# A chunked RWKV-7 block: the pair matrices from 64-column matmuls, and new written orders for the engines

## The reference

```python
xn = _layernorm(x)
s = attn(xn)                      # RWKV-7 time mixing
g = _silu(ffn(xn))                # ffn: down(silu(gate(xn)) * up(xn)), 256 -> 768 -> 256, int weights / 127
return x + s * g
```

```python
sa = einsum('bhij,bhj->bhi', S, at)
S = S * dt[:, :, None, :] + sa[..., None] * bt[:, :, None, :] + vt[..., None] * kt[:, :, None, :]
y = einsum('bhij,bhj->bhi', S, rt)
```

## Time and profile before

| | |
|---|---|
| median of 3 runs | 1602.91 us (1601.87 to 1603.78) |
| the profiled execution's own time | 1603.78 us |
| its span, first to last instruction | 1602.3 us |
| TensorE busy | 1493.2 us (93%) |
| VectorE busy | 1261.4 us (79%) |
| ScalarE busy | 1073.9 us (67%) |
| GpSimd busy | 335.8 us (21%) |
| mean granted TensorE clock | 0.982 |

### The profile page before, as it was taken

One profiled execution on the slowest core, in us unless ns is written; L12 is line 12 of the kernel. 1 busy time (PEld: TensorE's weight loads), 2 busy tenths in 40 slices (PEclk: granted clock), 3 DMA queues, 4 the chain that ended last, 5 costly groups with the idle time before them and its releaser, 6 DMA issues.

```text
span 1602.3 us, 56437 instructions
## 1 busy us (share of the span) xinstructions
PE 1493.2 (93%) x24384; PEld 1028.5 (64%) x24384; DVE 1261.4 (79%) x2661; ACT 1073.9 (67%) x1889; POOL 335.8 (21%) x362
## 2 busy tenths in 40 slices
PE   3579999999999999899999989999999999999977
PEld 1256767576676767667676666757666675766755
DVE  2788888888888888788887878888888888878623
ACT  3658587585858758576775858768585876858412
POOL 3020301313040131302213030131304013130101
PEclk9799999999999999999999999999999999999979
DMA  4011120301112030110302112030111203011110
GB/s 149 14 21 21 35 47 17 62 19 40 28 35 47 17 62 19 33 34 24 58 16 46 35 21 47 17 62 19 40 36 32 42 17 62 20 40 28 34 34 28
DMA packets 251462, 58.37 MB, mean 36 GB/s; under 512 B 223696, under 2 KB 250704, under 8 KB 251088
## 3 DMA queue, kind: packets, MB, share of 16 engines
q1 hardware_dynamic: 241936, 41.95, 13.8%
q10 hardware_dynamic: 9280, 12.81, 2.2%
HBM read 36.38 MB, written 18.35 MB: 34 GB/s over the span
## 4 chain that ended last, share of the span: by engine, by line
PE 85%; DVE 6%; issue 2%; DMA 2%; ACT 2%; POOL 1%; SPq 1%; ACTq 0%; DVEq 0%; POOLq 0%
PE bank L536 21%; PE chunk L380 15%; PE bank L546 10%; PE bank L511 4%; PE bank L666 3%; PE chunk L644 3%; PE chunk L616 3%; PE chunk L591 3%; PE chunk L600 3%; PE bank L479 2%; PE bank L519 2%; PE bank L485 2%; DMA smalls<-in_x 2%; PE chunk L630 2%; PE bank L380 2%
## 5 line engine op out<-in xcount | busy, mean ns | idle before, releaser
L1327 POOL TENSOR_TENSOR SF<-ST,CT 128x256 f32<-128x256 f32 x128 | 84.1, 657 | 678.3 <-DVE ST L1213 678.3
L536 PE MATMUL bank<-xT,wg 128*128 128x256 f32 x768 | 202.8, 396 | 13.4 <-DVE VU L983 13.4
L536 PE MATMUL bank<-xT,wu 128*128 128x256 f32 x768 | 201.7, 395 | 4.6 <-DVE hT L1173 4.6
L546 PE MATMUL bank<-wd,hT 128*128 128x256 f32 x768 | 177.2, 384 | 0.9 <-DVE hT L1173 0.9
L536 PEld LDWEIGHTS bank<-xT,wg 128*128 128x128 f32 x768 | 139.2, 191 | 58.7 <-DVE VU L983 24.0
L546 PEld LDWEIGHTS bank<-wd,hT 128*128 128x128 f32 x768 | 144.5, 192 | 27.7 <-issue 7.4
L536 PEld LDWEIGHTS bank<-xT,wu 128*128 128x128 f32 x768 | 139.2, 191 | 34.1 <-issue 7.9
L380 PE MATMUL chunk<-KS,W 128*128 128x512 f32 x320 | 151.1, 603 | 2.3 <-ACT gT L721 2.3
L863 ACT ACTIVATE sg<-bank 128x512 f32<-128x512 f32 x96 | 57.2, 595 | 137.3 <-PE bank L536 125.6
L889 ACT ACTIVATE Y<-chunk 32x256 f32<-32x256 f32 x256 | 96.0, 375 | 50.1 <-PE chunk L600 47.3
L380 PE MATMUL chunk<-big,W 128*112 128x512 f32 (+1 forms) x256 | 121.9, 600 | 2.9 <-POOL big L1286 2.6
(11 more groups left out here) (157 smaller groups left out, 3230.1 us busy)
## 6 DMA issues: line engine op xcount, KB each, us to landing
smalls<-in_x SPq DMA_DIRECT2D x32, 256.0 KB, 3.0
Y<-in_x SPq DMA_DIRECT2D x32, 256.0 KB, 3.0
out<-fsil ACTq DMA_DIRECT2D x32, 256.0 KB, 2.2
scrA<-AM SPq DMA_DIRECT2D x64, 64.0 KB, 1.9
hat<-scrB SPq DMA_DIRECT2D x32, 128.0 KB, 3.1
hat<-scrF SPq DMA_DIRECT2D x32, 128.0 KB, 3.3
KE<-scrA SPq DMA_DIRECT2D x64, 32.0 KB, 2.1
scrT<-KE SPq DMA_DIRECT2D x16, 128.0 KB, 1.7
```

Of the source, the lines that this page charges most:

```text
L536: q = pe.matmul(o[:, TT_ * n2:TT_ * n2 + TT_], w[:, h, 128 * (n + n2):128 * (n + n2) + 128], x_now[:, h], start=(h == 0), stop=(h == NH - 1))
L546: q = pe.matmul(o[:, 256 * m:256 * m + 256], hT[:, n, 128 * m:128 * m + 128], wd[:, n, :], start=(n == 0), stop=(n == NF - 1))
L1327: pool.tensor_tensor(SF[:, :, :, :], ST[:, :, :, :], fade[:, c].unsqueeze(3).to_broadcast([128, B, NH, N]), ALU.mult).then_inc(*faded.up)
```

## The change

In `pairs` the loop over the kind x goes, and one matmul takes the 64 columns of block j (both kinds of keys) as weights, so its output covers 64 partitions of the batch's half. The columns of K past 8j + 8 of each kind, which hold what earlier blocks or quarters left there, are multiplied too, and the mask leaves these places out as it did before. All three orders of PE, ACT and DVE are new, of POOL the string ORDER is new and the other two are as before; each string has the same number of each letter.

```diff
-ORDER = {"pe": ("NNNFNKOOFNNOKVONNNNKVKRRBKBNNRNNNBBNBBVBNNBVBBNBBEBNBBVBBNBBVBXBBNNBXBBNBBXBXBBNBBNBXBBXNBBLBXBBNXBB"
-                "LXXXXLL"),
-         "act": ("NFKFFFFFOFNNKVKOVKKKBERBKKXRRXDBXBNNVBVBBVVBNBBXBBBVXBBBVNBXBBXBBLBXLBLBBXNBBLXX"),
-         "dve": ("ONBOOBBBBBOBBDBBBBDBBDDBNBBOKKXFEDKDDDKNEEXKEEXBBXXNXBXXBXXXBXXXBEEXXBXXXXBNLBXBLXXBXBXXNXXXXXXBXBXB"
-                "LLXBBXLLLLLLLL"),
-         "pool": ("DBBBBBLBLBBBLLLLLLLL")}
+ORDER = {"pe": ("NNNFNKOOFNNORVNNNNKKOVKRBNKBNRNNVBBNBBNBNBNBBVNNBBEBVBBNBBVBNBBNBBXBXBBNXBBNBNBBXBBXBXBBNBBLBNBBXXBB"
+            "LXXXXLL"),
+         "act": ("NFKFFFFFRFVNKKNVOKKKBEBOKRKRDXXBXBVNBVNBBVVNBBBXBVVBBXBBBBNBBXXBLBBXLXBXBBNBBLXX"),
+         "dve": ("ONBOOBBBBBDBBBBBBBNBBDBBDDOOKKDXEFKKNDEDEXDKEEBXBXXXNBXBXXXBEXXBEXXBXNXBLXBXXXBXXBLXBXNXXXBXXXBXLXLBX"
+             "XXBBXXLLLLLLLL"),
+         "pool": ("DBBBBBBLBBLBLLLLLLLL")}
...
-LAST = {"pe": ("NNNNNONONNNOONNNBBNNNBBNBBBBBNBBBBBBNBBBBNBBBBBBNNBBBBBNBBBBNBBBBBBNBBNNNN"),
+LAST = {"pe": ("NOOONONNNNNNNNNBBNNNBBBBBNBBBBBNBBBBBNBBBBBNBBBNBBNBBBBBNBBBBBNBBBNBBNNNNN"),
...
-        "dve": ("BONOOBBBBBBBBBBBBBBBBONONBBBBBBBBNBBBNBBBBBNB"),
+        "dve": ("BOOOBBBBBBBBBBBBBBBBONONNBBBBBBBBBBBNBBBBBNBN"),
...
@@ -505,11 +505,9 @@
                     for n in range(QC // 2):
                         for j in range(NJ):
                             for b in range(B):
-                                for x in range(2):
-                                    p0, keys = 64 * b + L * x, BL * j + BL
-                                    oc = o[p0:p0 + keys, 128 * n:128 * n + 128].rearrange("p (x e) -> p x e", e=L)
-                                    q = pe.matmul(oc[:, :, BL * j:BL * j + BL], K[:, 2 * n + b, 64 * j + L * x:64 * j + L * x + keys],
-                                                  Q[:, 2 * n + b, j, :, :, :].rearrange("p a b e -> p (a b) e"), start=True, stop=True)
+                                oc = o[64 * b:64 * b + 64, 128 * n:128 * n + 128].rearrange("p (x e) -> p x e", e=L)
+                                q = pe.matmul(oc[:, :, BL * j:BL * j + BL], K[:, 2 * n + b, 64 * j:64 * j + 64],
+                                              Q[:, 2 * n + b, j, :, :, :].rearrange("p a b e -> p (a b) e"), start=True, stop=True)
                         if n == 1:
                             yield f"half{qt}"
                     q.then_inc(*ring.fill((t, "A", qt)))
```

More of the change, by code:

```diff
@@ L51 @@
 CTOT = _at
-ORDER = {"pe": ("NNNFNKOOFNNOKVONNNNKVKRRBKBNNRNNNBBNBBVBNNBVBBNBBEBNBBVBBNBBVBXBBNNBXBBNBBXBXBBNBBNBXBBXNBBLBXBBNXBB"
-                "LXXXXLL"),
-         "act": ("NFKFFFFFOFNNKVKOVKKKBERBKKXRRXDBXBNNVBVBBVVBNBBXBBBVXBBBVNBXBBXBBLBXLBLBBXNBBLXX"),
-         "dve": ("ONBOOBBBBBOBBDBBBBDBBDDBNBBOKKXFEDKDDDKNEEXKEEXBBXXNXBXXBXXXBXXXBEEXXBXXXXBNLBXBLXXBXBXXNXXXXXXBXBXB"
-                "LLXBBXLLLLLLLL"),
-         "pool": ("DBBBBBLBLBBBLLLLLLLL")}
-FIRST = {"pe": ("NNFKFVKKVNKNNRNNNRVKNNNNVNNNNVVREXNNXXXLXXNNXXNNXNLNNXXXLNLNN"),
-         "act": ("FKFFNFFFNKFNKNVVKKEKRVVVNKXDKRXVRXVXLVNXNLXLXXXXLNX"),
-         "dve": ("DNDDDDKKEDNDFDNKKNEENXXLKXEXXEXXEXXXXXXELXXXXXXXXXXXXXXXXNXXLLXXXXXLLLLLLLL"),
+ORDER = {"pe": ("NNNFNKOOFNNORVNNNNKKOVKRBNKBNRNNVBBNBBNBNBNBBVNNBBEBVBBNBBVBNBBNBBXBXBBNXBBNBNBBXBBXBXBBNBBLBNBBXXBB"
+            "LXXXXLL"),
+         "act": ("NFKFFFFFRFVNKKNVOKKKBEBOKRKRDXXBXBVNBVNBBVVNBBBXBVVBBXBBBBNBBXXBLBBLXLBXBBNBBLXX"),
+         "dve": ("ONBOOBBBBBDBBBBBBBNBBDBBDDOOKKDXEFKKNDEDEXDKEEBXBXXXNBXBXXXBEXXBEXXBXNBXLBXXXBXXBLXBXNXXXBXXXBXLXLBX"
+             "XXBBXXLLLLLLLL"),
+         "pool": ("DBBBBBBLBBLBLLLLLLLL")}
+FIRST = {"pe": ("NFKFKKNNNNNVNNKVRKRVNRVVNNNNNNNNNNNNNNNNNVEXXXNXXXLXXXXXLXLLN"),
+         "act": ("NNKFFFNFNNFFKFKVKKKEVKKRRXXDRVVVVVVXXXNNXNLXXLLXXLX"),
+         "dve": ("DNDDDNFKKEDNKKDXEXDDENKEXXXLEXXXXXXLXXXEXEXXXXXXXXNXXXXXXXXXXXLLXXLLLLLLLNL"),
          "pool": ("DLLLLLLLLLL")}
-LAST = {"pe": ("NNNNNONONNNOONNNBBNNNBBNBBBBBNBBBBBBNBBBBNBBBBBBNNBBBBBNBBBBNBBBBBBNBBNNNN"),
-         "act": ("NNNBBOBBBBOBBNBBBBBBBBNBNBBBBBBBBBNBN"),
-         "dve": ("BONOOBBBBBBBBBBBBBBBBONONBBBBBBBBNBBBNBBBBBNB"),
-         "pool": ("BBBBBBBBB")}
+LAST = {"pe": ("NOOONONNNNNNNNNBBNNNBBBBBNBBBBBNBBBBBNBBBBBNBBBNBBNBBBBBNBBBBBNBBBNBBNNNNN"),
+        "act": ("NONNOBBNBBBBBBBBNBBBBBBBBBNBBBBBBBBNN"),
+        "dve": ("BOOOBBBBBBBBBBBBBBBBONONNBBBBBBBBBBBNBBBBBNBN"),
+        "pool": ("BBBBBBBBB")}
 NB = 4
```

## The result

The changed kernel takes 1608.76 us (median of 10 runs, 1604.13 to 1614.75), the kernel before 1599.9 us beside it (10 runs, 1595.47 to 1605.19). The ratio is 1.0053, 95% interval 1.0037 to 1.0069: slower by 0.5%, some 8.5 us. The direction was forecast, but 45 us of it were expected, and 1608.76 lies outside the range of 1632 to 1662.

The account below looks back on a forecast made before the run. TensorE (PE), busy 1493.2 of 1602.3 us, was taken as the bound. 1603.8 + 44.9 (pair matmuls) + 1.5 (tile 0) - 1.5 (orders) = 1648.7 us, against the median 1648 us; range 1632 to 1662 us.

Parts of the forecast that it names:

- the round: Pair matmuls: records running side by side, four per 33 ns before, forecast two per 58 ns with 64 weight columns.
- The twin at line 573: Corner product with 32 records, two strips and 64 weight columns; its 1.11 us was taken as the new half's length.
- the half: Pair matmuls of half a quarter, 8 per tile: alone 0.74 us before, 1.11 us forecast.
- Rival B: Pair matmuls: the round stays at 33 ns, so no change, 1603 us; 3 in 100.
- time added to or taken from a PE stage in the steady sections passes to the end nearly one for one: Steady sections: 2.99 us more matmul time in each of 15 sections was to give +44.9 us.
- rival A: Pair matmuls: a price for each record makes the half 0.27 us, total 1571 or 1591 us; 7 in 100.
- 30.7 us of idle time: PE's free time in 1200 us of steady sections, about 2.4 us a section, taken to bound the new orders' gain.
- rival D: Group norm on VectorE meets GpSimd's mixes in five sections more, some 4 us each: 1668 us; 7 in 100.
- I take -1.5 us over all: Written orders of all four engines: the longer last row of two covers 0.77 us of each of two group-norm waits.
- nothing within 3 us: Last section, which has no pairs: its new order was taken as worth nothing, within 3 us.
- 65 changes of shape: PE's steady order: 65 changes of matmul shape before and afterwards, each costing a like drain, so no effect.
- C: Steady sections: the new orders close all PE idle time and hide the longer halves, 1612 us; 3 in 100.

Follow-up runs that it names:

- experiment 1: The changed kernel's 64-column matmuls with all written orders of the kernel before: 1624.37 us, ratio 1.0134 to the kernel before.
- experiment 5: Changed kernel with one old string each: ORDER 1614.17 us, FIRST 1612.61, LAST 1619.18; kernel before with new ORDER alone: 1646.99 us.

## Why the prediction was wrong

**Right.** PE bounds the kernel. 64 weight columns set the round at 58 ns for two records. The twin at line 573 gave the half to 0.01 us (1.11 forecast, 1.12 measured), and two experiments moved the round with the columns (29 ns at up to 32, 48 ns in the mean of 40 to 64). LDWEIGHTS lasts 138 ns where 133 was forecast. Rival B, a round that stays at 33 ns, is out. The direction, slower, was right.

**The step that failed: "time added to or taken from a PE stage in the steady sections passes to the end nearly one for one".** It was shown wrong by experiment 1: +44 us of stage time gave +21. The largest part of what is missing that the traces can assign is what the removed records had cost elsewhere: the narrow halves used up PE's fetched instructions. Of the 20 stalls, 3 stood inside the pairs and their transposes and 17 in the recurrence stages behind them. The sum had put this at nothing. I had priced the instruction count only inside the half, in rival A, where it costs nothing. The trace before held the signs, in the same view as the earlier trace rows, of which I had used only the waits for VectorE:

```profile
PE chunk L630 <- issue: 3.5, 7, 0.9
...
PE chunk L600 <- issue: 1.4, 3, 0.8
PE bank L511 <- issue: 0.7, 1, 0.7
```

None of these stages begins with such a wait for data; it stands in their middle. A gap shorter than the 0.2 us that a matmul's record lasts is hidden as busy time, so that 30.7 us of idle time was no bound on what PE could win back. Of the 26.1 us that experiment 1 wins back in 14 sections of the traces (42.1 less 16.0), stalls of over 0.18 us are 10.6 and the group norm's waits 5.8. Behind one of these waits, of 2.7 us, the clock before fell to half its level:

```profile
671.00:679.00 8.00, 8.00 (x31) 4.71 (x30) 5.30 (x18) 5.25 (x7) 0.00 (x0) 0.57 0.21 66
```

The stages from line 420 to the next of line 666 took 7.3 us there, and the same stages 4.1 us in the trace of experiment 1. Another 3.0 us lie ahead of line 644, which in the trace before waits for VectorE's VU for 2.4 us in five places. The last 3.5 us are not assigned.

**The group norm's wait** in the steady sections was part of the profiled execution before and of none of the twelve others, with old or new orders (rival D's mechanism, in the other direction). One trace can't tell whether every execution of the kernel before has it. My forecast started from a median of 1602.9 us for three runs, where ten gave 1599.9: 3 us of the 39 us error.

**"I take -1.5 us over all" for the orders.** They are worth 1.0134 - 1.0053, 13 us, and by the times the largest part lies in FIRST and LAST, which I had put at nothing within 3 us. That is the second failed term. Some 6 of the 13 us, by the estimate of experiment 5, are a higher clock outside the steady sections, which the prediction did not price at all. ORDER, which I had called neutral by its 65 changes of shape, is neutral within the intervals when the matmuls are wide. I also miscounted it: the new string has two rows of two halves in a section, since half2 and matrix2 are adjacent too, which saves one switch, 0.2 us. The prediction's last paragraph would have put an error with halves as forecast on the orders, to be seen in PE's waits for other engines. The larger part was in the matmuls after all, and its sign was the waits that went.

**The sum as it was:** 1600 + 44 (halves) - 23 (stalls, waits, clock and gaps that went) - 13 (orders) = 1608 us, against 1608.76 measured. The 23 is the 44 less experiment 1's 21, so that the sum must come out; measured by themselves in the traces are 10.6 us of stalls, 5.8 of waits and 3.2 of clock.

**The rivals.** A was wrong as put: the half did not get shorter with its record count. But a price for records was there, outside the half: 10.6 us of stalls. C named the place where a part of the time went (PE's idle time) and held it to be 36 us; 1612 us was its figure, nearer than the forecast. That was luck: it needed every wait of the earlier trace rows gone, and the 10.7 us for the mixes are all still there, with 17.3 of the 30.7 free us.

## What to carry to other kernels

When PE is busy for 97% of a stretch, look for waits marked "issue" in the middle of its stages before pricing a change in the number of matmuls: the instructions have to be fetched, and a dense burst of small matmuls is paid for where the block ends, in the burst or in the stage behind it. Counting PE's records modulo 256 finds the place. Busy time made of overlapping records hides every gap shorter than one record; sum the times from start to start instead. A written order belongs to the matmuls it was made with: the same strings were worth -13 us with one form of the matmuls and +32 us with the other, so test them as a pair.

## What the runs showed of the hardware beyond this

PE resumed 1.2 to 1.6 us after the landing of a 16 KB block of instructions in 19 of 20 gaps of the kernel before, and 1.61 us after it in the twentieth. The blocks themselves took 0.9 to 1.9 us, mostly about 1, and in the thirteen traces none started sooner than 3.2 us after the last. By the count of records, PE had at most some 300 records in hand when the fetch of a block began (212 in the median before), so the fetch was about one block ahead of it. A round of two records took 29 ns in the mean at 8 to 32 weight columns, 48 ns in the mean at 40 to 64, and 58 ns at 64, the last with weights of 128 rows (line 509, 32 moving columns) as with weights of 64 rows (line 573, 16 moving columns).
